# Input weights by transposing a weighed table, and kernel numbers as running sums, in a long-convolution and gated-expert kernel

## The reference, cut to what matters

```python
K = 2.0 * jnp.einsum('hn,hnl->hl', Cs, jnp.exp(P)).real      # Cs = C * (exp(dtA) - 1) / A, P = dtA * l
y = irfft(rfft(u_m, 2 * L) * rfft(K, 2 * L))[..., :L]
y = (y + u_m * D[:, None]) * mask[:, None, :]
logits = einsum('bsd,ed->bse', y, route_w)                   # top one of E = 8
h = einsum('bsd,erd->bser', y, A)
out = x + einsum('bser,eor->bso', one_hot(top) * top * h, Bw)
```

## Time and profile before

| | us |
|---|---|
| median of three runs | 609.56 |
| lowest and highest | 608.71, 609.94 |
| the profiled execution | 609.9 |
| its span in the trace | 608.1 |

### The profile page before, as it was taken

How to read it: one execution, slowest core, us unless ns; L and a number is a source line. 1 busy time by engine, 2 the same in 40 slices (tenths; PEclk the granted TensorE clock), 3 DMA queues, 4 the chain that set the end, 5 groups by cost and what they waited for, 6 DMA issues and landing times.

```text
span 608.1 us, 13318 instructions
## 1 busy us (share of the span) xinstructions
PE 581.6 (96%) x3617; PEld 529.0 (87%) x3617; DVE 490.3 (81%) x1371; ACT 317.2 (52%) x1059; POOL 385.9 (63%) x520
## 2 busy tenths in 40 slices
PE   3589999999999999999999999999999999999996
PEld 3478999999999989999999999999999999999984
DVE  7768888887888888788888888888888888887875
ACT  3666754555465455546545554664555456445420
POOL 4668657666765766676575667657566765665430
PEclk9999999999999999999999999999999999999999
DMA  6212454454345344434534443453444345445422
GB/s 119 73 54 86 149 155 98 144 155 125 120 148 156 100 141 153 125 119 148 157 96 143 153 135 110 148 157 97 143 152 132 114 147 157 102 139 151 138 85 83
DMA packets 37582, 77.64 MB, mean 128 GB/s; under 512 B 12476, under 2 KB 20862, under 8 KB 37510
## 3 DMA queue, kind: packets, MB, share of 16 engines
q1 hardware_dynamic: 28358, 43.76, 28.8%
q10 hardware_dynamic: 9152, 33.03, 13.3%
HBM read 43.16 MB, written 33.62 MB: 126 GB/s over the span
## 4 chain that ended last, share of the span: by engine, by line
PE 92%; DVE 3%; ACT 2%; issue 1%; POOL 1%; DMA 0%; ACTq 0%; POOLq 0%
PE psYo L1060 20%; PE psZ L1080 19%; PE psO L1060 15%; PE psYe L1060 13%; PE psS L1060 11%; PE psO L1107 5%; PE psXe L1071 5%; PE psXo L1071 5%; PE psZ L1136 1%; DVE psS L918 0%; DVE ex L758 0%; DMA logs<-in_L_cond_log_dt_dram 0%; POOL both L465 0%; DVE ost L957 0%; ACT L577 0%
## 5 line engine op out<-in xcount | busy, mean ns | idle before, releaser
L504 POOL TENSOR_TENSOR Slo<-Sf,Shi 128x384 fp32r<-128x384 f32 x64 | 65.3, 1021 | 166.1 <-ACT Shi L651 166.1
L918 DVE SCALAR_TENSOR_TENSOR psS<-Sf,tab,psS 64x128 f32<-64x128 f32 x256 | 91.9, 359 | 48.1 <-ACT Sf L646 41.2
L1080 PE MATMUL psZ<-Wt,Y 128*128 128x136 f32 x1024 | 129.2, 279 | 0.0
L1080 PEld LDWEIGHTS psZ<-Wt,Y 128*128 128x128 f32 x1024 | 123.3, 190 | 0.1
L646 ACT ACTIVATE Sf<-psS 128x128 f32<-128x128 f32 x64 | 17.8, 277 | 200.3 <-PE psS L1060 200.3
L957 DVE TENSOR_TENSOR ost<-psO,xt 128x512 f32<-128x512 f32 x128 | 87.7, 690 | 1.2 <-PE psO L1060 1.1
L497 POOL TENSOR_TENSOR Xlo<-xeven,Xhi 128x512 fp32r<-128x512 f32 x64 | 82.9, 1295 | 0.0
L465 POOL TENSOR_TENSOR both<-coarse,fine 128x512 f32<-128x512 f32 x64 | 69.0, 1079 | 1.3 <-ACT fine L591 1.2
L941 DVE TENSOR_TENSOR wlo<-psZ,whi 128x128 fp32r<-128x128 f32 x64 | 18.7, 292 | 41.2 <-ACT whi L656 41.2
L1060 PE MATMUL psYo<-Xhi,Thi 128*128 128x512 f32 x128 | 51.2, 400 | 0.0
L1060 PE MATMUL psYo<-Xlo,Thi 128*128 128x512 f32 x128 | 51.1, 399 | 0.0
(11 more groups left out here) (193 smaller groups left out, 1522.2 us busy)
## 6 DMA issues: line engine op xcount, KB each, us to landing
xt<-in_x_dram SPq DMA_DIRECT2D x64, 512.0 KB, 4.9
out_dram<-ost ACTq DMA_DIRECT2D x63, 512.0 KB, 5.1
Traw<-kdram SPq DMA_DIRECT2D x64, 128.0 KB, 2.9
kdram<-krow SPq DMA_DIRECT2D x64, 1.0 KB
A_nat<-in_L_ffn_A_dram SPq DMA_DIRECT2D x1, 512.0 KB, 5.1
B_nat<-in_L_ffn_Bw_dram SPq DMA_DIRECT2D x8, 64.0 KB, 3.5
out_dram<-ost SPq DMA_DIRECT2D x2, 256.0 KB, 2.0
lens_i<-in_itok_B_dram SPq DMA_DIRECT2D x1, 64.0 KB, 5.0
```

The source lines that it names most:

```text
L504: pool.tensor_tensor(Slo[h.s2][:, :], Sf[h.s2][:, :], Shi[h.s2][:, :].bitcast(F32), ALU.subtract).then_inc(slo_done, 1)
L918: dve.scalar_tensor_tensor(psS[to, new], Sf[h.s2][fr, old], tab2[fr, BR, h.n:h.n + 1], psS[to, new], ALU.mult, ALU.add).then_inc(brought_d ...
L1080: last = pe.matmul(psZ[:, 0:NW], Y[:, j, c, :], Wt[:, 2 * c + j, :], start=(j == 0 and c == 0), stop=(j == 1 and c == NE - 1), skip_group_ ...
```

## The change

Mx and its constant go, and with them the fp32 products. Instead the table W, whose two halves transposed are B, is made as a whole: `cross_parts` on ScalarE copies Grev to same with a scale per partition (MA), and each half of 64 partitions of Grev to the other half of cross, with the scale MB; `w_table` on GpSimd adds the two to Wg; `inputs` transposes the two halves of Wg. The kernel numbers are the sums of the rows of psB over its first 64 columns: `b_hi` takes them as accumulators of two ScalarE copies. They are shifted by one position, so that the number at distance zero (the sum of CK, and D) is a value of its own, K0, which VectorE works out once in pack2; kcol and krow get a third block, which also brings the zeros that were written to HBM at the start. In ScalarE's step m_matrix goes from behind first_state, cross_parts stands behind g_hi, and w_hi stands ahead of turns and mirror, not behind them. In GpSimd's step w_table stands behind g_lo. scrap is written and not read.

```diff
             def write_kernel(h):
-                sp.dma_start(bass.AP(kdram.tensor, h.s2 * (P + Q), [[G32, P // G32], [P, 2], [1, G32]]),
+                sp.dma_start(bass.AP(kdram.tensor, h.s2 * (P + Q), [[G32, P // G32], [P, 3], [1, G32]]),
                              krow[h.s2][0:P:G32, :, :]).then_inc(k_out[h.s2], 16)
             def skew_kernel(h):
-                             bass.AP(kdram.tensor, h.s2 * (P + Q), [[1, P], [1, Q]])
+                             bass.AP(kdram.tensor, h.s2 * (P + Q) + 1, [[1, P], [1, Q]])
...
-            sp.wait_ge(zero_row, 2)
-            sp.dma_start(Dcol[P - 1:P, :], D.rearrange("(a h) -> a h", a=1)).then_inc(in_D, 16)
-            for s in range(2):
-                sp.dma_start(kdram[s:s + 1, Q:Q + P], zeros[:, :]).then_inc(pad_done, 16)
+                sp.dma_start(D_nat[:, :], D.rearrange("(h a) -> h a", a=1)).then_inc(in_D, 16)
...
             def g_table(h):
-                need(pool, b_mm, h.n - 1)
+                need(pool, crossed, (h.n - 1) * 3)
...
+            def w_table(h):
+                need(pool, crossed, h.n * 3 + 3)
+                need(pool, b_mm, h.n - 1)
+                pool.tensor_tensor(Wg[h.s2][:, :], same[:, :], cross[:, :], ALU.add).then_inc(wg_done, 1)
...
                 if head(3).there:
                     g_lo(head(3))
+                    w_table(head(3))
...
             g_table(first[0])
+            w_table(first[0])
             g_table(first[1])
             g_lo(first[0])
+            w_table(first[1])
             g_table(first[2])
...
             x_lo(first[1])
+            w_table(first[2])
             turn_parts(parts[1])
             g_table(first[3])
             g_lo(first[2])
+            w_table(first[3])
             weigh(parts[1])
...
-            def m_matrix(h):
-                need(act, b_mm, h.n - 1)
-                for j, table in enumerate((M0, M1)):
-                    act.activation(Mx[h.s2][:, j * N:(j + 1) * N], twin[:, j * N:(j + 1) * N], ACT.Copy,
-                                   scale=col(tab2[:, table, :], h)).then_inc(mx_done, 1)
-                act.activation(Mx[h.s2][:, P:P + 1], col(tab2[:, CK, :], h), ACT.Copy).then_inc(mx_done, 1)
+            def cross_parts(h):
+                need(act, grev_done, h.n + 1)
+                need(act, wg_done, h.n)
+                act.activation(same[:, :], Grev[h.s2][:, :], ACT.Copy, scale=col(tab2[:, MA, :], h)).then_inc(crossed, 1)
+                for to, fr in ((slice(0, N), slice(N, P)), (slice(N, P), slice(0, N))):
+                    act.activation(cross[to, :], Grev[h.s2][fr, :], ACT.Copy,
+                                   scale=tab2[fr, MB, h.n:h.n + 1]).then_inc(crossed, 1)
             def b_hi(h):
-                act.activation(kcol[h.s2][:, 0, 0:1], psB[:, 0, P:P + 1], ACT.Copy).then_inc(kcol_done, 1)
-                act.activation(kcol[h.s2][:, 1, 0:1], psB[:, 1, P:P + 1], ACT.Identity,
-                               bias=Dcol[:, h.n:h.n + 1]).then_inc(kcol_done, 1)
+                need(act, kcol_done, h.n * 3)
+                for j in range(2):
+                    act.activation(scrap[:, j, :], psB[:, j, 0:N], ACT.Copy,
+                                   accum_out=kcol[h.s2][:, j, 0:1]).then_inc(kcol_done, 1)
+                act.activation(kcol[h.s2][:, 2, 0:1], col(tab2[:, K0, :], h), ACT.Copy).then_inc(kcol_done, 1)
...
-                if head(3).there:
-                    m_matrix(head(3))
...
                 if head(3).there and not is_head(head(0), 1):
                     g_hi(head(3))
+                    cross_parts(head(3))
+                if head(-1).there:
+                    w_hi(head(-1))
                 if part_at(head(7)):
                     turns(part_at(head(7)))
                 if part_at(head(4)):
                     mirror(part_at(head(4)))
-                if head(-1).there:
-                    w_hi(head(-1))
...
-            m_matrix(first[0])
+            act.wait_ge(b_turned, 1)
+            act.activation(Bw_hi[:, 0:512], psY[0][:, :], ACT.Copy).then_inc(bhi_set, 1)
+            cross_parts(first[0])
...
             sines(parts[1])
-            m_matrix(first[3])
+            cross_parts(first[3])
             t_hi(first[1])
             g_hi(first[3])
             mirror(parts[1])
...
-            link(TT(pack2[:, CK, 0, :], prod[:, 0, 0, :], prod[:, 1, 1, :], ALU.subtract), 1)
-            link(TT(pack2[:, CK, 1, :], prod[:, 0, 1, :], prod[:, 1, 0, :], ALU.add))
+            link(TT(CK[:, 0, :], prod[:, 0, 0, :], prod[:, 1, 1, :], ALU.subtract), 1)
+            link(TT(CK[:, 1, :], prod[:, 0, 1, :], prod[:, 1, 0, :], ALU.add))
+            link(dve.reduce_sum(ksum[:, :], CK[:, 0, :], axis=AX.X), 1)
...
+            TT(pack2[:, K0, 0, 0:1], ksum[:, :], D_nat[:, :], ALU.add).then_inc(pack2_done, 1)
...
             def inputs(h):
-                need(pe, mx_done, h.n * 3 + 3)
-                need(pe, grev_done, h.n + 1)
+                need(pe, wg_done, h.n + 1)
                 for j in range(2):
-                    last = pe.matmul(psB[:, j, :], Grev[h.s2][:, j * P:(j + 1) * P],
-                                     Mx[h.s2][:, :], start=True, stop=True, skip_group_check=True)
+                    last = pe.transpose(psB[:, j, :], Wg[h.s2][:, j * P:(j + 1) * P], ident[:, :])
                 last.then_inc(b_mm, 1)
```

More of the change, by code:

```diff
@@ L56, in conv_ffn_kernel @@
         ident = sb("ident", [P, P])
-        twin = sb("twin", [P, P])
         grid16 = sb("grid16", [P, G16])
@@ L64, in conv_ffn_kernel @@
         mask = sb("mask", [P, 2, NE, P])
-        zeros = sb("zeros", [1, P])
-        Dcol = sb("Dcol", [P, H])
+        D_nat = sb("D_nat", [H, 1])
         route_nat = sb("route_nat", [E, L])
@@ L77, in conv_ffn_kernel @@
         V, VH, VL, RHO = range(4)
-        LR, M0, M1, BR, CK = range(5)
+        LR, MA, MB, BR, K0 = range(5)
         pack1 = sb("pack1", [H, 4, 2, N])
@@ L108, in conv_ffn_kernel @@
         CA = sb("CA", [H, 2, N])
+        CK = sb("CK", [H, 2, N])
+        ksum = sb("ksum", [H, 1])
         warm = sb("warm", [P, 1])
@@ L134, in conv_ffn_kernel @@
         Glo = [sb(f"Glo{s}", [P, Q], F32R) for s in range(4)]
-        Mx = [sb(f"Mx{s}", [P, P + 1]) for s in range(2)]
-        kcol = [sb(f"kcol{s}", [P, 2, G32]) for s in range(2)]
-        krow = [sb(f"krow{s}", [P, 2, G32]) for s in range(2)]
+        same = sb("same", [P, Q])
+        cross = sb("cross", [P, Q])
+        Wg = [sb(f"Wg{s}", [P, Q]) for s in range(2)]
+        scrap = sb("scrap", [P, 2, N])
+        kcol = [sb(f"kcol{s}", [P, 3, G32]) for s in range(2)]
+        krow = [sb(f"krow{s}", [P, 3, G32]) for s in range(2)]
         Bhi = [sb(f"Bhi{s}", [P, 2, P], F32R) for s in range(2)]
@@ L165, in conv_ffn_kernel @@
         psO = [bank("psO0"), bank("psO1")]
-        psB = psO[0][:, :].rearrange("p (j w) -> p j w", j=2)[:, :, 0:P + 1]
+        psB = psO[0][:, :].rearrange("p (j w) -> p j w", j=2)[:, :, 0:P]
         psWh = psZ[:, 384:384 + P]
@@ L176, in conv_ffn_kernel @@
         in_B = sem("in_B")
-        pad_done = sem("pad_done")
         consts = sem("consts")
         cols_set = sem("cols_set")
-        zero_row = sem("zero_row")
         v_set = sem("v_set")
@@ L218, in conv_ffn_kernel @@
         glo_done = sem("glo_done")
-        mx_done = sem("mx_done")
+        crossed = sem("crossed")
+        wg_done = sem("wg_done")
         b_mm = sem("b_mm")
@@ L361, in _ @@
             sp.dma_start(route_nat[:, :], route_w).then_inc(in_rw, 16)
-            sp.wait_ge(zero_row, 2)
-            sp.dma_start(Dcol[P - 1:P, :], D.rearrange("(a h) -> a h", a=1)).then_inc(in_D, 16)
-            for s in range(2):
-                sp.dma_start(kdram[s:s + 1, Q:Q + P], zeros[:, :]).then_inc(pad_done, 16)
+            with nc.allow_non_contiguous_dma(reason="64 numbers"):
+                sp.dma_start(D_nat[:, :], D.rearrange("(h a) -> h a", a=1)).then_inc(in_D, 16)
             with nc.allow_non_contiguous_dma(reason="expert rows of 16"):
@@ L373, in _ @@
             load_x(Head(2))
-            sp.wait_ge(pad_done, 32)
             for n in range(3):
@@ L389, in _ @@
         def _(pool):
-            pool.memset(zeros[:, :], 0.0).then_inc(zero_row, 1)
-            pool.memset(Dcol[:, :], 0.0).then_inc(zero_row, 1)
             pool.memset(ident[:, :], 0.0).then_inc(consts, 1)
-            pool.memset(twin[:, :], 0.0).then_inc(consts, 1)
             pool.iota(grid16[:, :], pattern=[[-1, G16]], base=G16 - 1, channel_multiplier=0,
@@ L399, in _ @@
                       allow_small_or_imprecise_dtypes=True).then_inc(consts, 1)
-            pool.wait_ge(consts, 5)
+            pool.wait_ge(consts, 4)
             pool.affine_select(out=ident[:, :], in_=ident[:, :], compare_op=ALU.not_equal, fill=1.0,
[L403 to L410, removed]
                                base=0, pattern=[[-1, P]], channel_multiplier=1).then_inc(consts, 1)
@@ L558, in _ @@
```

(34 more changed lines are left out.)

## The result

| | before | after |
|---|---|---|
| median, us | 609.14 (608.71 to 609.94) | 646.61 (646.26 to 647.91) |
| the profiled execution's span, us | 608.1 | 646.1 |
| mean of the 59 steps from the third Sf on, us | 8.86 | 9.41 |

The changed kernel is slower: ratio 1.0618, interval 1.0603 to 1.0633. The steps are the distances between the 64 starts of Sf in ScalarE's timeline, of which the first lies in the written-out start; after, three of four take 9.34 and the fourth 9.62. Of the 38.0 us between the spans, 32.5 lie between the third Sf (51.91 before, 56.01 after) and the last (591.77 and 628.32), 4.1 ahead of it, and 1.4 behind it.

What follows compares the result with a forecast made beforehand. TensorE was taken to bound the kernel before, and ScalarE's late whi to set the step after. The profiled 609.9 us plus 23.0 for the steady loop and 5.4 for the start gave 638 us, range 615 to 648.

Steps and rivals of the forecast that it cites:

- The bound and the place: Steady loop: TensorE runs without gaps before the change; afterwards it waits ahead of up, about 0.5 to 0.6 us a step.
- a whi behind 5.30: ScalarE, us after Sf: latest whi start without lengthening the step, read where mirror copies stand between Ghi and whi.
- TensorE's gain: Steady loop: inputs and its transposes shrink, 0.23 us a step, so the loop could run at 8.62.
- cross_parts: ScalarE between Ghi and whi: three scaled copies make that stretch 1.79 us, whi starts at 5.65, the step reaches 9.20.
- VectorE's fractions: VectorE in one step of four: fractions behind the adds make carry 0.17 us late, 0.04 in the mean.
- nothing changes at the end: End of the kernel, with no head left to prepare: no added time.
- The running sums: b_hi on ScalarE: two sums and a one-column copy, up to about 1.0 us, covered by removed work and idle time: zero.
- The start: Before the steady loop: cross_parts and w_table delay the first heads, 5.4 us in all, between 3.5 and 7.5.
- The second: Rival on cross_parts: all three copies overlap as those over 128 partitions do, whi at 5.40, 623 us; chance 0.18.
- the third: Rival on cross_parts: copies run at 0.31 us each, the scale column free, whi at 5.10, 604 us; chance 0.13.
- The fourth: Rival on b_hi: running sums cost over 0.5 us each, Shi is late too, 656 us at 0.65 each; chance 0.05.

Runs made afterwards that it cites:

- the copies alone: Kernel before plus three unread copies of Grev between Ghi and whi, turns and mirror moved behind whi: 639.04 us, ratio 1.0476.
- the fractions alone: Changed kernel with whi ahead of cross_parts, and GpSimd waiting in one step of four for VectorE's fractions before g_table: 602.64 us, ratio 0.9882.

## Why the prediction was right, point by point

**The bound and the place.** That a whi behind 5.30 makes the step longer was read from the mirror step; the run with the copies alone, and the exchange of whi and cross_parts, show it from both sides. That whi gates up is what the 30.0 us of TensorE's wait say, 0.51 us in each of 59 steps. The mechanism was right and the sizes were too small: the forecast loss was 28 us, the measured 37.5, which is only just inside the 9 us allowed around 638. Two terms of the loop make up most of the difference.

**TensorE's gain** of 0.23 us a step was sized right: 8.64 where the loop is free again (forecast 8.62), and the changed kernel could not collect it.

**cross_parts** was the first term too small. Forecast was 1.79 us from Ghi to whi; it took 1.90 (323.36 to 325.26). same, the two cross copies' lengths (0.507 by the groups by line, forecast 0.52) and the missing overlap between them came out as worked from the mirror copies. The last 0.10 did not: I let whi overlap the second cross copy, as it had overlapped the last mirror copy, and that copy wrote the other half of the partitions; with the order exchanged, whi overlaps again. From 5.65 to 5.76 that is 0.11 of the 0.14 by which the plain step, 9.34, is over the forecast 9.20. The rest I didn't trace.

Of "ScalarE: Activation LUTs" (the Trainium skill, section "What ACT_TABLE_LOAD costs"), weighed in the prediction, the price of the scale column and the rate hold here too (same took 0.50). Its overlap of back-to-back copies differs: same to the first cross copy took 0.52 us, not 0.40, and it held in these runs only where the second copy starts at partition 0 on both sides and the first one writes from partition 0.

**VectorE's fractions** were the second term too small: 0.17 late each fourth step forecast, 0.28 measured. I took frac's two operations at their old 0.73, inside the 3.75 of the earlier trace rows, which already held a wait for GpSimd:

```profile
308.23 0.73 DVE L863 SCALAR_TENSOR_TENSOR frac<-step_l,frac 128x64 f32<-128x64 f32 x2
```
```profile
307.99 0.74 POOL L475 TENSOR_TENSOR Grev<-both 128x256 f32<-128x256 f32 x1
```

In the changed kernel Grev starts at 328.19, just ahead of frac at 328.24, and the pair takes 0.90:

```profile
328.24 0.90 DVE L864 SCALAR_TENSOR_TENSOR frac<-step_l,frac 128x64 f32<-128x64 f32 x2
```
```profile
328.19 0.74 POOL L463 TENSOR_TENSOR Grev<-both 128x256 f32<-128x256 f32 x1
```

I had costed w_table at nothing since GpSimd has time; but its place in the queue puts Grev onto the whole of frac: it takes 0.7 us ahead of both and Grev there, and with the copies alone Grev was done in time. "SBUF — State Buffer", section "Who interferes with whom", of the Trainium skill has the rule (a VectorE instruction with two SBUF inputs contends with a GpSimd instruction that reads SBUF), and the run with the fractions alone agrees for frac, which has two: its pair falls from 0.79 to 0.35. fraction, which reads one tile, fell from 0.64 to 0.23 as well; that rule doesn't cover it.

Together 0.11, 0.03 (not traced) and 0.03 (a fourth of 0.11) make the loop's 0.55 a step out of the forecast 0.39: 59 x 0.17 = 10 us, less 1.3 for the start (below), which leads from 638 to 646.7, where the median is 646.6. That nothing changes at the end did not hold in the profiled execution, at 647.9 the longest of the four: it took 1.4 us more there, 1.2 of them in its last six products (last section).

**The running sums** cost nothing, as taken: one has 0.23 us for the copy and 0.21 for the read of the accumulator, which start 0.10 apart, and Shi's idle time grew from 0.34 to 0.51.

```profile
320.75 0.23 ACT L614 ACTIVATE scrap<-psO 128x64 f32<-128x64 f32 x1
320.85 0.21 ACT L614 ACTIVATION_READ_ACCUMULATOR scrap<-psO 128x1 f32 x1
```

**The start** was forecast at 5.4 and took 4.1; the first Sf of the loop came at 46.76, where near 48 was expected. inputs of head 0 came 2.2 late (26.01; forecast 2.3). At weigh the delay was 3.5 (44.86 after, 41.34 before), not 4.6: inputs takes about half as long in each of the three first heads, and TensorE's within of head 0 ran faster at first (its first products started 0.32, 0.23 and 0.30 us apart, where they were 0.57, 0.42 and 0.43 apart before), so the sines came only 1.4 late. I had carried the first delay on unchanged. w_table of head 3 put weigh 2.1 us further behind the sines (forecast 2.3). Head 4 cost 0.8 (forecast 0.7), but in another place: the first step of the loop took 9.25 where it was 8.45, since the Sf behind it (56.01) came as cross_parts of head 4 ended. The wait of inputs for Wg of head 4, 1.02 us, fell into the next step, which took 9.34 like the others. Moving these gave 3 us back.

**The rivals.** The second (all copies overlap) and the third (a free scale column) fall with the rows of cross. The fourth (sums) falls with the run without them.

## What to carry to other kernels

In this kernel, work moved from the full engine to one with idle time was free only behind what the full engine waits for. Ask of each idle gap what ends it, and whether the operation behind the gap is one that the full engine needs next: here the 0.93 us gap stood in front of such a one, and one exchange in the list was worth 37 us. A step in which something else already stands in that gap shows how much it holds. Ask too what the new work pushes back in its own queue: in the loop w_table made nobody wait for GpSimd, and still made the fractions on VectorE slower.

## What the runs showed of the hardware

- Among these copies on ScalarE, a copy that read or wrote from partition 64 did not start under the one before it (same to a straight copy at partition 0: 0.40 us; to one that reads from 64: 0.52), and none started under a copy that wrote from 64. Behind a copy that read from 64 and wrote from 0 a next one that started at partition 0 overlapped by 0.10 us (whi 0.95 behind the first cross copy, not 1.07).
- A VectorE operation of 0.23 us with one input (fraction) took 0.64 beside GpSimd's additions, and a pair with two inputs each 0.79 to 0.90 instead of 0.35; the wait lies inside the instruction's row.
- In the changed kernel's last six products the granted clock was 0.53 of full speed, so close to the lower of its two levels (1.2 and 2.4 GHz), and the stretch behind the last Sf took 17.8 us where it took 16.3 before (the six products 2.8 and 1.6). The columns are stretch, length, busy time of five engines, granted clock, transfer share and GB/s:

```profile
628.00:636.00 8.00, 7.74 (x46) 6.58 (x45) 6.00 (x16) 1.08 (x3) 1.00 (x1) 1.00 0.16 66
636.00:639.60 3.60, 1.54 (x12) 1.15 (x10) 1.52 (x7) 0.28 (x1) 0.00 (x0) 1.00 0.36 146
639.60:642.40 2.80, 2.75 (x6) 1.71 (x6) 0.69 (x1) 0.00 (x0) 0.00 (x0) 0.53 0.00 0
```

TensorE had waited 1.38 us and then 0.74 just ahead of them, exactly as in the kernel before, where the clock stayed at 1.00. The last products were slow (0.63 us for 512 columns, not 0.39) in four of the ten profiles, among kernels of both kinds, so the change is not shown to be the cause.
